# Moving the scatters and the blank fills of a routing table within an attention stage

## The reference

```python
x = x + _L0_xattn_ref(_layernorm(x), ctx_1024, ctx_1024, ...)   # 16 heads of 16
x = x + _L0_ffn_ref(_layernorm(x), ...)

# in _L0_ffn_ref: 32 experts in 8 groups, 4 experts per token
shared = silu(xf @ sg) * (xf @ su) @ sd
_, top_group_idx = top_k(group_scores, 4)
top_scores, top_idx = top_k(masked, 4)
gates = softmax(top_scores)
capacity = 250
pos = cumsum(onehot, axis=0)[..., flat_e] - 1      # place of a token in its expert
keep = pos < capacity
# expert e works on its 250 slots; a token gets gate * result of its 4 experts
return shared + routed
```

## Time and profile before

| | us |
|---|---|
| median of 3 runs | 1789.15 (1788.22 to 1790.02) |
| profiled execution, own time | 1794.52 |
| its span | 1792.5 |
| PE busy in the span | 1497.2 (84%) |
| POOL busy | 461.1 (26%) |
| scatters into `row_token` (64, L3101) | 64.3 busy |
| first and last scatter start | 479.0 and 672.6 |

### The profile page before, as it was taken

How to read it: one execution, slowest core, us unless ns; L and a number is a source line. 1 busy time by engine, 2 the same in 40 slices (tenths; PEclk the granted TensorE clock), 3 DMA queues, 4 the chain that set the end, 5 groups by cost and what they waited for, 6 DMA issues and landing times. The chain is left out here.

```text
span 1792.5 us, 30479 instructions
## 1 busy us (share of the span) xinstructions
PE 1497.2 (84%) x11670; PEld 1128.7 (63%) x11670; DVE 799.8 (45%) x2278; ACT 687.3 (38%) x1423; POOL 461.1 (26%) x437
## 2 busy tenths in 40 slices
PE   3989987698888799999999936988699999819992
PEld 2556554366655566888888823655467666619991
DVE  4665562467675432222222215666556766511111
ACT  1543542565554411222222212455555555503330
POOL 0221210011233353656666420111101111040003
PEclk9999998699998899999999967899899999959996
DMA  6433422977665123778778644455566776229993
GB/s 244 131 100 120 139 85 86 166 130 125 119 107 102 48 57 85 200 201 201 189 192 205 163 109 97 97 125 124 94 128 111 118 119 113 33 92 356 346 340 90
DMA packets 255033, 254.98 MB, mean 142 GB/s; under 512 B 117532, under 2 KB 228468, under 8 KB 249396
## 3 DMA queue, kind: packets, MB, share of 16 engines
q1 hardware_dynamic: 210868, 222.04, 49.0%
q0 software_dynamic: 41152, 28.50, 8.5%
q10 hardware_dynamic: 2880, 2.62, 0.4%
HBM read 195.67 MB, written 57.20 MB: 141 GB/s over the span
## 5 line engine op out<-in xcount | busy, mean ns | idle before, releaser
L2637 PE MATMUL cross_ps_score<-cross_q,cross_k 128*128 128x250 f32 x1024 | 223.5, 376 | 0.8 <-DVE cross_q L3052 0.8
L2637 PEld LDWEIGHTS cross_ps_score<-cross_q,cross_k 128*128 128x128 f32 x1024 | 195.6, 191 | 23.9 <-DVE cross_q L3052 1.0
L3061 DVE TENSOR_TENSOR cross_prob<-cross_act_,cross_ps_score 128x250 f32<-128x250 f32 x128 | 53.2, 416 | 268.3 <-ACT cross_act_ L2757 263.8
L3140 POOL DMA_INDIRECT x_sum<-cross_ye,cross_token x64 | 128.6, 2009 | 80.8 <-ACT cross_ye L2763 68.7
L1656 ACT ACTIVATE layer_parts<-layer_ps_prob 128x400 f32<-128x400 f32 (+1 forms) x192 | 96.9, 508 | 102.7 <-PE layer_ps_prob L1479 100.9
L2784 DVE TENSOR_REDUCE cross_nmax<-cross_ps_score 100x2 f32<-100x722 f32 x128 | 112.2, 904 | 48.7 <-PE cross_ps_score L2404 45.1
L2667 ACT ACTIVATE cross_prob<-cross_ps_prob 128x400 f32<-128x400 f32 (+1 forms) x192 | 94.7, 505 | 76.1 <-PE cross_ps_prob L2438 72.3
L2649 PE MATMUL cross_ps_prob<-cross_val,cross_prob 128*125 128x256 f32 x512 | 115.8, 379 | 0.0
L2757 ACT ACTIVATE cross_act_<-cross_ps_score 128x250 f32<-128x250 f32 x128 | 48.5, 379 | 167.6 <-PE cross_ps_score L2637 166.2
L2649 PEld LDWEIGHTS cross_ps_prob<-cross_val,cross_prob 128*125 128x125 f32 x512 | 93.5, 188 | 12.8
L3130 POOL DMA_INDIRECT cross_xe<-ln_rows,cross_token x64 | 79.7, 1245 | 81.8 <-PE cross_ps_misc L2623 57.6
(11 more groups left out here) (397 smaller groups left out, 2945.9 us busy)
## 6 DMA issues: line engine op xcount, KB each, us to landing
experts_w<-in_w SPq DMA_DIRECT2D x40, 1024.0 KB, 7.1
k_stack<-mixer_part SPq DMA_DIRECT2D x32, 541.5 KB, 3.5
cross_k<-in_wg SPq DMA_DIRECT2D x32, 512.0 KB
cross_k<-in_wu SPq DMA_DIRECT2D x32, 512.0 KB
cross_val<-in_wd SPq DMA_DIRECT2D x32, 512.0 KB
cross_k<-k_stack SPq DMA_DIRECT2D x32, 270.8 KB
layer_stacks<-k_stack SPq DMA_DIRECT2D x32, 270.8 KB, 5.1
mixer_ctx<-in_ctx_t POOLq DMA_DIRECT2D x16, 361.0 KB, 4.1
```

Source lines behind the costliest of these rows:

```text
L2637: ins = nc.tensor.matmul(ps_pre[m][:, side, 0:CAP], w[s][:, k, m * P:(m + 1) * P], xt[s][:, k, :], start=(k == 0), stop=(k == KD - 1))
L3140: g.indirect_dma_start(prog.x_sum, bass.IndirectOffsetOnAxis(token[:, 2 * e + t:2 * e + t + 1], 0), ye[s][:, t, :], None, compute_op=ALU.a ...
```

## The change

The scatters of group 0 go out in steps 14 and 15, eight in each (four ahead of `root` and `inverse_length`, four behind). Group 1's sixteen follow behind them, four ahead of `root(15)`, four ahead of `inverse_length(15)`, eight behind, and then come groups 2 and 3. POOL's wait for the blanks moves from ahead of step 0 to step 14. SP issues the three fills in step 4 counted from 0, the fifth, behind the first half of the loads for sequence 6. POOL's wait for the fill of `x_sum` moves ahead of the first gathers.

```diff
+    BLANKS_AT = G
...
-                sp.wait_ge(zero_set, 1)
-                sp.dma_start(prog.row_token[0:SLOTS0].rearrange("(p n) o -> p (n o)", p=T),
-                             blank[:].rearrange("p n o -> p (n o)")).then_inc(zeroed, 16)
-                sp.wait_ge(blank_set, 1)
-                sp.dma_start(prog.ln_rows[N:N + CAP].rearrange("(t p) d -> p t d", p=HALF), xe[0][:]).then_inc(blank_rows, 16)
-                sp.dma_start(prog.x_sum[N:N + CAP].rearrange("(t p) d -> p t d", p=HALF), xe[0][:]).then_inc(blank_sums, 16)
                 for b in range(B):
...
                         load_half(b + 2, 0)
+                    if b == BLANKS_AT:
+                        sp.wait_ge(zero_set, 1)
+                        sp.dma_start(prog.row_token[0:SLOTS0].rearrange("(p n) o -> p (n o)", p=T),
+                                     blank[:].rearrange("p n o -> p (n o)")).then_inc(zeroed, 16)
...
                     if b > 0:
                         store_rows(b - 1)
...
                 set_base(0)
-                g.wait_ge(zeroed, 16)
                 for b in range(B):
                     if b + 1 < B:
                         set_base(b + 1)
-                    if b >= 2 * G:
-                        scatter(b // G - 2, b % G * TOPK, TOPK // 2)
+                    if b == B - 2:
+                        g.wait_ge(zeroed, 16)
+                    if b >= B - 2:
+                        scatter(0, (b - (B - 2)) * 2 * G, G)
                     if b > 0:
                         root(b - 1)
                         inverse_length(b - 1)
-                    if b >= 2 * G:
-                        scatter(b // G - 2, b % G * TOPK + TOPK // 2, TOPK // 2)
-                scatter(NG - 2, 0, G)
+                    if b >= B - 2:
+                        scatter(0, (b - (B - 2)) * 2 * G + G, G)
+                scatter(1, 0, G)
                 root(B - 1)
-                scatter(NG - 2, G, G)
+                scatter(1, G, G)
                 inverse_length(B - 1)
-                scatter(NG - 2, 2 * G, 2 * G)
+                scatter(1, 2 * G, 2 * G)
+                scatter(NG - 2, 0, 4 * G)
                 scatter(NG - 1, 0, 4 * G)
...
                 g.wait_ge(blank_rows, 16)
+                g.wait_ge(blank_sums, 16)
...
                 g.wait_ge(shared_stored, NG * 16)
-                g.wait_ge(blank_sums, 16)
```

More of the change, by code:

```diff
@@ L2355, in _ @@
                         load_half(b + 2, 0)
+                    if b == BLANKS_AT:
+                        sp.wait_ge(zero_set, 1)
+                        sp.dma_start(prog.row_token[0:SLOTS0].rearrange("(p n) o -> p (n o)", p=T),
+                                     blank[:].rearrange("p n o -> p (n o)")).then_inc(zeroed, 16)
+                        sp.wait_ge(blank_set, 1)
+                        sp.dma_start(prog.ln_rows[N:N + CAP].rearrange("(t p) d -> p t d", p=HALF), xe[0][:]).then_inc(blank_rows, 16)
+                        sp.dma_start(prog.x_sum[N:N + CAP].rearrange("(t p) d -> p t d", p=HALF), xe[0][:]).then_inc(blank_sums, 16)
                     if b > 0:
```

## The result

The changed kernel takes 1799.66 us (median of 20 runs, 1791.84 to 1816.13) where the kernel before took 1789.64 (20 runs, 1782.43 to 1798.01) beside it: ratio 1.0076, 95% interval 1.0050 to 1.0102. It is slower, by 10.0 us in the medians. The prediction said 1785, faster, and 1795 as its upper end. The runs after lie on two levels, eleven from 1791.84 to 1800.16 and nine from 1808.26 to 1816.13. Between the two spans only 1.3 us are left.

The account below looks back on a forecast made before the run. It took PE, busy 84% of the span and slow through short instructions while POOL scatters, as the bound. Its terms, -15.8 + 3.9 + 5.6 + 2.8 - 0.5 = -4.0, gave 1785 us, range 1776 to 1795.

Parts of the forecast that it names:

- Part 1: Steps 8 to 13: without their 24 scatters the six intervals take 98.9 us instead of 114.6, -15.8.
- Part 2: Steps 14 and 15: later root and a burst of eight scatters delay PE, +3.9 us (+1.7 to +8.5).
- Part 3: From root(14) to the turned table: scatters end later, so the table is ready later, +5.6 us (+3.8 to +7.5).
- Part 4: Behind the table wait: PE, idle 7.1 us instead of 1.46, then runs at half clock, +2.8 us (0 to +3.4).
- Part 5: Fills moved from the start to step 4: a key wait goes, later loads pay, -0.5 us (-2 to +3).
- B: Rival, steps 14 and 15: PE is held as long as eight scatters last, sum +0.6, 1790 us; chance 0.20.
- C: Rival, steps 8 to 13: long intervals are not the scatters' doing, little gained, 1801 us; chance 0.17.

Follow-up runs that it names:

- none: The kernel before without the 24 scatters of steps 8 to 13 (entries missing): 1775.57 us, ratio 0.9928.
- blanks: The kernel before with only the fills moved to step 4, scatters as before: 1784.83 us, ratio 0.9972.
- rootfirst: The changed kernel with root ahead of the first four scatters in steps 14 and 15: 1807.08 us, ratio 1.0072 to the kernel before.
- again: The changed kernel once more, nothing edited: 1794.57 us, ratio 1.0034 to the kernel before.
- again2: The changed kernel once more in another job, nothing edited: 1803.93 us, ratio 1.0067 to the kernel before.
- hold: The changed kernel, POOL waiting after four of group 2's scatters until group 3's rows are ready: 1794.91 us, ratio 1.0020 to the kernel before.
- short: The changed kernel without the last 12 of group 2's scatters (entries missing): 1784.29 us, ratio 0.9946 to the kernel before.
- moved: The changed kernel without its move of the fills, which stay at the start: 1780.56 us, ratio 1.0061 to the kernel before.
- direct: The kernel before with the 24 scatters of steps 8 to 13 as plain DMAs of 100 rows from POOL's queue: ratio 0.9968.

## Why the prediction was wrong

**Part 1** was right: steps 8 to 14 forecast at 98.9 us, measured 97.4, -17.2 for -15.8. The remote waits are gone, as said. `none` has 98.5. Against the 110.5 of `blanks`, which has scatters there too, the saving is 13.1, so the size hangs on which profile one takes. It is right for the jobs in which PE is held: in the other, these steps take 97.5 with their scatters, and there is nothing to save.

**Part 2** was right in kind and a little small: +5.7 to root(14), forecast +3.9 within 1.7 and 8.5. The eight scatters hold ACT 2.72 us at 582.55 and 6.29 at 591.99. PE runs at 0.50 from 585.2 to 598.9, where it did so for 6.8 us before, and part 2 had no term for that. By `rootfirst` some 2.7 is the late root, forecast 1.7.

**Part 3** is the step that failed. Forecast was +5.6 from root(14) to the table (+3.8 to +7.5), with group 3's scatters without idle time ahead. Measured was +16.9 (89.36 against 72.42), with 6.38 idle ahead of them; it is +15.4 in `again` and +25.5 in `again2`. Nearly all of it, 15.9, lies behind root(15). The working counted only POOL's queue and took PE's side as given, on the ground of the earlier trace rows: PE untroubled beside scatters where its instructions are long.

Two things were wrong in it. First, I read the 10.01 us of the earlier trace rows in which POOL idled as slack, and filled them. With that the row ahead of group 3's scatters grew from 18 (616.66 to 643.21) to 36 (600.78 to 649.10), and rows so long hold long matmuls too: `again2`, `hold` and `rootfirst` show it. `short`, which cuts the row to 24, takes most of the loss back. The fourteen place matmuls of group 3, 0.20 us each, which had stood in that pause, came to stand inside the row, and their signal to DVE came 19 us late. Second, does not carry what I laid on it. Its window from 640 to 660 holds the whole pause, 643.2 to 653.2, so only half of its 20.00 busy us are beside scatters. PE was indeed not held beside the 16 that follow, up to 673.57, but nothing there speaks of a longer row. Where PE is not held, in the job of `moved`, the same working gave +4.3, within its range.

**Part 4** did not come: PE's wait ahead of the table stayed 1.46, since PE was late itself. Instead the clock fell within the hold: its mean is 0.90 from 611.0 to 655.5, where it was 1.00 in the like stretch before.

**Part 5** was too small: -4.3 in the profile (-4.4 over twenty profiles) for -0.5, outside its range of -2 to +3. It was priced by the two waits for keys near the fills alone, and left out the clock behind them. Between the adds of steps 0 and 1 before, PE waits 0.9 us for keys, the mean clock is 0.94 and the step takes 18.99 us; after, it waits for none, the clock is 1.00 and the step takes 16.52. In `none`, with the fills at the start too, the wait is 3.8, the clock 0.84 and the step 21.1, so the profile of before was one of the milder ones. From the rule of the Trainium skill that I weighed there ("DMA: Bandwidth & Descriptors", Queues, rings and completion order), that descriptors are taken in ring order, I had worked out that the loads behind the fills start later, at 2.4 us more if they had no slack. It seems that they had: in the profile after, steps 1 to 8 take 111.2 us against 112.9 (473.66 - 362.44, 477.97 - 365.11), so no such loss shows.

**The sum.** In the profiled pair: -4.3 - 17.2 + 5.7 + 1.0 + 15.9 + 0.2 = +1.3 for a forecast of -4.0. The medians make it +10.0, because the execution profiled before was one of its slower ones and that after not one of the upper level, near 1812. Of the rivals, B (the stall moves along) was nearest in kind; but it placed the stall in steps 14 and 15, at 1790, and the one that decided is 25 us further on. C came nearest in number, 1801, by luck: it had the long intervals not the scatters' doing, and they were. The bad ends of all parts came to +13.0, about 1802; the range was cut at 1795, and no part and no rival had PE held behind root(15).

## What to carry to other kernels

A row of indirect transfers from GpSimd is not free because it lies off the critical path: in five of six jobs here TensorE was held beside it, at short instructions after one or two, at long ones for more than 1.1 us at a time only in rows of 24 and more (those of 16 and 18 did not). In this kernel such transfers in fours beside long matmuls, with the short ones behind them, did not hold it; that order alone was worth 1.0%, where gathering them into one long row cost 0.3 to 0.8% with the fills' gain in it. And before work is put into an idle stretch of one engine, list what the others do in it, for the idleness may be what lets them through; and check that a window that is to show two things side by side does not hold the pause between them.

## What the hardware showed that was not expected

- While held, PE starts one matmul per 1.40 us (`hold`) or per 2.1 to 2.8 us (`rootfirst`), against 0.34 each at full speed (10.91 us for 32), with scatters 1.29 apart. PE's signals are late by up to 19 us besides. Why, is open: no engine that the profile shows is in its way, and plain transfers of as many rows from the same queue do not do it (`direct`).
- The same kernel took 1789.6 to 1794.5 in five jobs and 1771.4 in a sixth, whose profiles show no hold; that job and one of the five were on a chip of the same number. Span and granted clock were recorded in every execution here, so no run tells whether PE is held when nothing is recorded.
- Executions spread more where PE is held: 1791.8 to 1816.1 over 20 runs of the change, 1783.3 to 1797.1 over 29 of the kernel before, against 1766.3 to 1776.1 over 21 of the latter in the job without holds. That they differ by which instructions get through before a hold is a guess from two profiles, that of the change and that of `rootfirst`.
